# A two-layer language-model tower on one core: in the first attention, the diagonal masks of the key-major scores move from GpSimd to TensorE

## What is computed

```python
Q, K, V = (proj(W_Q), proj(W_K), proj(W_V))        # 8 sequences, 16 heads of 16 features, 512 tokens
Q = _apply_rope(Q, cos, sin)
K = _apply_rope(K, cos, sin)
scores = jnp.einsum('bhsd,bhtd->bhst', Q, K) / jnp.sqrt(jnp.float32(D_K))
scores = jnp.where(causal[None, None], scores, -jnp.inf)
attn = jax.nn.softmax(scores, axis=-1)
out = jnp.einsum('bhst,bhtd->bhsd', attn, V)
```

## Time and profile before

| | us |
|---|---|
| median of 3 runs (lowest to highest) | 1921.43 (1909.6 to 1924.99) |
| the profiled execution, own time | 1921.16 |
| its span, first to last instruction | 1919.4 |
| first attention, PE's first product to the end of the stage | 438.3 (219.3 to 657.6) |
| granted TensorE clock, whole span / this stage | 0.80 / 0.64 of 2.4 GHz |

### The profile page before, as it was taken

One profiled execution on the slowest core, in us unless ns is written; L12 is line 12 of the kernel. 1 busy time (PEld: TensorE's weight loads), 2 busy tenths in 40 slices (PEclk: granted clock), 3 DMA queues, 4 the chain that ended last, 5 costly groups with the idle time before them and its releaser, 6 DMA issues. The chain is left out here.

```text
span 1919.4 us, 30959 instructions
## 1 busy us (share of the span) xinstructions
PE 1405.3 (73%) x9797; PEld 1029.2 (54%) x9798; DVE 956.5 (50%) x1884; ACT 636.3 (33%) x1175; POOL 716.1 (37%) x703
## 2 busy tenths in 40 slices
PE   0599399999999746524442299646599699999997
PEld 0287254444444444423331177544589688888886
DVE  0677665555555254557778255463544233333332
ACT  0177044434344412223221044312233233333332
POOL 6144566656641201113444500200174135454454
PEclk9799566666666777867766599877799899999999
DMA  1034866555531000014323244022011363444431
GB/s 28 18 132 176 238 204 197 162 178 172 191 108 35 7 7 0 0 51 119 99 82 105 63 103 103 10 79 80 6 28 32 113 222 55 114 112 114 112 55 26
DMA packets 123069, 179.31 MB, mean 93 GB/s; under 512 B 26100, under 2 KB 84028, under 8 KB 122980
## 3 DMA queue, kind: packets, MB, share of 16 engines
q1 hardware_dynamic: 94420, 117.25, 20.0%
q0 software_dynamic: 28560, 60.91, 12.3%
HBM read 104.76 MB, written 74.31 MB: 93 GB/s over the span
## 5 line engine op out<-in xcount | busy, mean ns | idle before, releaser
L1378 DVE TENSOR_REDUCE att_top<-att_psS 128x4 f32<-128x512 f32 (+2 forms) x192 | 198.2, 1044 | 176.7 <-PE att_psS L1273 176.0
L1349 ACT ACTIVATE att_prob<-att_psS 128x1024 f32<-128x1024 f32 (+1 forms) x192 | 169.1, 884 | 265.9 <-PE att_psS L1287 265.9
L2427 POOL DMA_INDIRECT out<-ffn1c_y,ffn1c_table x72 | 114.3, 1587 | 181.6 <-ACT ffn1c_y L2540 122.2
L1314 PE MATMUL att_psO<-att_prob,values 128*17 128x512 f32 (+3 forms) x1024 | 146.1, 659 | 10.4 <-ACT att_outT L1355 10.4
L1267 PE MATMUL att_psS<-att_ka,att_qa 48*128 48x384 f32 (+3 forms) x512 | 130.9, 515 | 29.8 <-DMA att_shut<-att_shut 26.1
L1200 POOL TENSOR_SCALAR_AFFINE_SELECT att_prob<-att_prob 128x512 f32<-128x512 f32 x128 | 81.2, 637 | 186.5 <-ACT att_prob L1349 181.4
L1267 PEld LDWEIGHTS att_psS<-att_ka,att_qa 48*128 48x128 f32 x512 | 66.9, 258 | 126.9 <-issue 65.3
L1287 PE MATMUL att_psS<-att_qa,att_ka 50*128 50x256 f32 (+3 forms) x512 | 116.7, 499 | 15.4 <-DVE att_top L1378 13.4
L2568 DVE TENSOR_TENSOR ffn1c_hid<-ffn1c_psG,ffn1c_sil 128x512 f32<-128x512 f32 x72 | 49.8, 691 | 146.0 <-PE ffn1c_psG L2468 146.0
L2468 PE MATMUL ffn1c_psG<-ffn1c_w_h,ffn1c_xh 128*128 x288 | 99.2, 427 | 8.9 <-DMA ffn1c_w_l<-experts_lo 2.9
L2416 POOL DMA_INDIRECT ffn1c_rows<-normed_rows,ffn1c_table x72 | 70.8, 984 | 77.5 <-DVE ffn1c_gate L2588 53.7
(11 more groups left out here) (378 smaller groups left out, 3617.2 us busy)
## 6 DMA issues: line engine op xcount, KB each, us to landing
prep_raw<-in_w_all POOLq DMA_DIRECT2D x27, 512.0 KB, 3.8
experts_hi<-prep_hi POOLq DMA_DIRECT2D x27, 512.0 KB, 4.0
experts_lo<-prep_lo POOLq DMA_DIRECT2D x27, 512.0 KB, 5.7
ffn1c_w_h<-experts_hi SPq DMA_DIRECT2D x8, 1536.0 KB, 6.5
ffn1c_w_l<-experts_lo SPq DMA_DIRECT2D x8, 1536.0 KB, 10.7
qkv_near<-near_keys SPq DMA_DIRECT2D x32, 320.0 KB, 4.4
q_parts<-qkv_part SPq DMA_DIRECT2D x8, 1024.0 KB, 3.9
k_parts<-qkv_part SPq DMA_DIRECT2D x16, 512.0 KB, 5.2
```

The costliest lines, as they stand in the source:

```text
L1314: mm = pe.matmul(psO[VW * h:VW * h + DK + 1, P * j:S], va[:, TG * b + j, :, HG * hg + h], prob[:, w % 2, h, START[j]:START[j] + S - P * j] ...
L1349: act.activation(dst, src, ACT.Exp, scale=0.25).then_inc(s["exp"], 1)
L1378: dve.tensor_reduce(dst, src, AX.X, ALU.max).then_inc(s["max"], 1)
L2427: pool.indirect_dma_start(out=rows_out, in_=y[:, t.buf, :], in_offset=None, out_offset=bass.IndirectOffsetOnAxis(ap=table[:, t.value:t.val ...
```

## The change

- `key_scores` gets mask products of its own: after each pair of score products four products of 64 rows x 128 columns in bf16, `half` against a new constant `sooner`, on the 128 queries of the diagonal block. That is 8 groups of four in a unit, 1,024 products in all, as many as the query side has. POOL's 128 selects and the signal `tri` go; PE's value products wait for the exponential itself.
- The value products have 32 columns in place of 17. They read 15 columns beyond their own, so `va` has one more tile, which POOL clears in `project_rope`; the results of these columns land in rows of `psO` that nobody reads. `psO` need not be cleared any more.
- `half`, `later` (the former `shut`) and `sooner` are made in the identity's block at the program's start, all 128 rows, on POOL: three memsets and six selects. SP's two copies and PE's wait for them go.
- DVE writes the rows of -1 for two buffers ahead of the first round, and for the other four in rounds 0 to 3, two memsets ahead of the maxima of the round.
- POOL's pieces are paced by the maxima: piece u waits for all maxima of unit u - 1.

```diff
-            pool.memset(va[:, :, DK, :], 1.0).then_inc(s["ones"], 1)
+            pool.memset(va[:, NT], 0.0).then_inc(s["ones"], 1)
+            pool.memset(va[:, 0:NT, DK, :], 1.0).then_inc(s["ones"], 1)
...
-            for u in range(NU + 3):
-                if u < n_pieces:
-                    piece(pool, u)
-                v = u - 3
-                if 0 <= v < NU:
-                    for j, through in enumerate((2, 4, 5, 6)):
-                        tri = prob[:, v % 2, :, START[j]:START[j] + P]
-                        pool.wait_ge(s["exp"], 6 * v + through)
-
-                        pool.affine_select(out=tri, in_=tri, compare_op=ALU.is_ge, fill=0.0, base=0,
-                                           pattern=[[0, HG], [1, P]], channel_multiplier=-1).then_inc(s["tri"], 1)
+            for u in range(n_pieces):
+                if u >= 1:
+                    pool.wait_ge(s["max"], 6 * u)
+                piece(pool, u)
...
-            sp.wait_ge(s["mask"], 2)
-            for dst in (half, shut):
-                sp.dma_start(dst[64:128], dst[0:64]).then_inc(s_copied, 16)
...
                     for g in range(2):
                         r = slice(64 * g, 64 * g + QROWS + MROWS)
...
+                    for part in range(2):
+                        for g in range(2):
+                            r = slice(64 * g, 64 * g + 64)
+                            mm = pe.matmul(psS[:, bank, g, col:col + P], half[r, part, :], sooner[r, part, :],
+                                           start=False, stop=True, tile_position=(64 * g, 0), skip_group_check=True)
                 mm.then_inc(s["scoresB"], 1)
...
+            flat = va[:].rearrange("p t d h -> p (t d h)")
...
-                pe.wait_ge(s["tri"], TG * w + j + 1)
+                pe.wait_ge(s["exp"], 6 * w + (2, 4, 5, 6)[j])
...
-                    mm = pe.matmul(psO[VW * h:VW * h + DK + 1, P * j:S], va[:, TG * b + j, :, HG * hg + h],
+                    first = (TG * b + j) * (DK + 1) * H + HG * hg + h
+                    mm = pe.matmul(psO[VW * h:VW * h + VW, P * j:S], flat[:, first:first + VW * H:H],
...
-            pe.wait_ge(s_copied, 32)
-            pe.wait_ge(s["clear"], 1)
...
-            dve.memset(psO[:], 0.0).then_inc(s["clear"], 1)
-            for at in range(LOADED):
+            def minus_rows(at):
                 for g in range(2):
                     dve.memset(ka[64 * g + 32:64 * g + 64, at].bitcast(F32), -1.0).then_inc(s["minus"], 1)
+
+            for at in range(AHEAD):
+                minus_rows(at)
             for u in range(NU + 5):
+                if AHEAD <= u + AHEAD < LOADED:
+                    minus_rows(u + AHEAD)
...
+                for x in marks:
+                    pool.memset(x[:], 0.0).then_inc(s_id, 1)
+                pool.wait_ge(s_id, 5)
+                for g in range(2):
+                    rows = slice(64 * g, 64 * g + 64)
...
+                        pool.affine_select(out=x[rows], in_=x[rows], compare_op=compare, fill=fill, base=0,
+                                           pattern=pattern, channel_multiplier=step).then_inc(s_id, 1)
+                pool.wait_ge(s_id, 11)
```

More of the change, by code:

```diff
@@ L1148, in pair_order, with attend_pairs @@
     return out
-def attend_pairs(nc, q_dram, k_dram, m_dram, ident, va, split):
+def attend_pairs(nc, q_dram, k_dram, m_dram, ident, marks, va, split):
     NU = B * NHG
@@ L1161, in attend_pairs @@
     place = {what[1:]: n for n, what in enumerate(order)}
+    half, later, sooner = marks
     with ExitStack() as ctx:
@@ L1172, in attend_pairs @@
         psO, psM = k.ps("psO", [P, 512]), k.ps("psM", [P, 512])
-        s = {n: k.sem(n) for n in "blank mask minus clear scoresA max topT_ps topT scoresB exp tri pv outT turned rec norm".split()}
+        s = {n: k.sem(n) for n in "minus scoresA max topT_ps topT scoresB exp pv outT turned rec norm".split()}
         s_load = [k.sem(f"load{n}") for n in range(LOADED)]
         s_m_out, s_m_in = ([k.sem(f"{name}{n}") for n in range(2)] for name in ("m_out", "m_in"))
-        s_copied = k.sem("copied")
         block = ctx.enter_context(nc.Block())
@@ L1272, in query_scores @@
                             r = slice(64 * g, 64 * g + 64)
-                            mm = pe.matmul(psS[:, bank, g, col + cols - P:col + cols], half[r, part, :], shut[r, part, :],
+                            mm = pe.matmul(psS[:, bank, g, col + cols - P:col + cols], half[r, part, :], later[r, part, :],
                                            start=False, stop=True, tile_position=(64 * g, 0), skip_group_check=True)
@@ L1286, in key_scores @@
                         r = slice(64 * g, 64 * g + QROWS + MROWS)
-                        mm = pe.matmul(psS[:, bank, g, col:col + cols], ka[r, v % LOADED, q, P * j:P * (j + 1)],
-                                       qa[r, v % LOADED, q, P * j:S], start=True, stop=True, tile_position=(64 * g, 0),
-                                       skip_group_check=True)
+                        pe.matmul(psS[:, bank, g, col:col + cols], ka[r, v % LOADED, q, P * j:P * (j + 1)],
+                                  qa[r, v % LOADED, q, P * j:S], start=True, stop=True, tile_position=(64 * g, 0),
+                                  skip_group_check=True)
+                    for part in range(2):
[3 more added lines that the diff above has]
+                                           start=False, stop=True, tile_position=(64 * g, 0), skip_group_check=True)
                 mm.then_inc(s["scoresB"], 1)
@@ L2615, in tower @@
         ident = k.sb("ident", [P, P])
+        marks = [k.sb(name, [P, 2, P], BF16) for name in ("half", "later", "sooner")]
         s_id = k.sem("ident")
@@ L2632, in _ @@
                                    pattern=[[-1, P]], channel_multiplier=1).then_inc(s_id, 1)
-                pool.wait_ge(s_id, 2)
+                for x in marks:
[3 more added lines that the diff above has]
+                    rows = slice(64 * g, 64 * g + 64)
+                    for x, compare, fill, pattern, step in ((marks[0], ALU.not_equal, 1.0, [[-64, 2], [1, P]], -1),
+                                                            (marks[1], ALU.is_ge, MASKED, [[64, 2], [-1, P]], 1),
+                                                            (marks[2], ALU.is_ge, MASKED, [[-64, 2], [1, P]], -1)):
+                        pool.affine_select(out=x[rows], in_=x[rows], compare_op=compare, fill=fill, base=0,
+                                           pattern=pattern, channel_multiplier=step).then_inc(s_id, 1)
+                pool.wait_ge(s_id, 11)
         embed(nc, res, ident, s_rows, a["ids"], a["E1"], a["tok_w2t"], a["b2"], a["pos"])
-        with nc.sbuf_tensor("values0", [P, NT, DK + 1, H], F32) as va:
+        with nc.sbuf_tensor("values0", [P, NT + 1, DK + 1, H], F32) as va:
             project_rope(nc, res, ident, a["w_qk0"], a["w_v0"], (a["cos"], a["sin"]), q0_dram, k0_dram, va)
```

10 lines of the change are left out of this document (1 added, 9 removed).

## The result

| | kernel before | changed kernel |
|---|---|---|
| median (lowest to highest), us | 1922.69 (1909.6 to 1924.99) | 1858.67 (1858.34 to 1862.87) |
| profiled execution, own time / span | 1921.16 / 1919.4 | 1858.51 / 1856.7 |
| first attention, PE's first product to the end | 438.3 (219.31 to 657.6) | 376.9 (216.38 to 593.3) |
| granted clock, span / this stage | 0.80 / 0.64 | 0.87 / 0.93 |

The ratio is 0.9688, 95% interval 0.9651 to 0.9724: 62.7 us between the two profiled executions.

The account below looks back on a forecast made before the run. PE was taken to bound the first attention, its clock being the largest quantity. From 1921.2 us, -35 (units, clock) - 8 (constants) + 5 (memsets) + 3.5 (identity's block) = -34.5 gave 1887 us, range 1856 to 1917.

Parts of the forecast that it names:

- The bound: First attention: PE bounds it, its clock alternating; the high level is lost at waits for DVE's maxima in steps 5, 0, 1.
- The share at the high level: First attention: 2.4 GHz share rises from 25% to two thirds, units 12.5 us against 13.65, -35 us over 32.
- The forecast's own formula: First attention's mean unit time: 1 / (0.667/11.1 + 0.333/17.0) = 12.5 us, from the high-clock share and unit length at each level.
- the first rival: First attention: masks fill every weak place, full clock throughout, all units 11.1 us, -82 us for units; 1840 us, chance 0.08.
- Unit lengths: First attention, with all masks on the path: 11.1 us a unit at 2.4 GHz, 17.0 at 1.2 GHz; before, 10.47 and 15.2.
- The bounds given for half of the masks hidden: First attention's units, if half of the mask products is hidden: 10.5 us at 2.4 GHz and 16.6 at 1.2 GHz.
- Constants: Start of first attention: PE no longer waits for copies of mask constants, -8 us, or -5 if loads take 6.6 us.
- Memsets: Rounds 1 to 3: DVE's memsets between maxima cost 7.1 us, partly offset by unit 3's load wait; +5 (1.5 to 7).
- The identity's block: Program start: three memsets and six selects ahead of the embedding's gathers, all on the path, +3.5 us.
- POOL, and 32 columns: First attention: removing 128 selects gains 0; value products of 32 columns cost 0, by a 109 ns median weight load elsewhere.
- The old rhythm: First attention: masks thin the value products, high-clock share stays 25%, units 15.0 us, +43 us; 1964 us, chance 0.10.
- The transfers: First attention: faster units wait for loads, 3.18 us every third unit, 35 us, gain gone; about 1920 us, chance 0.08.

Follow-up runs that it names:

- experiments 1 and 3: Changed kernel with POOL's selects back: no key-side mask products, ratio 0.9979; all, 0.9653 (1). Masks in steps 4 and 5 only, 0.9632; steps 0 to 3 only, 0.9883 (3).
- experiment 4: Changed kernel with mask constants made in the projection, 1851.82 us; ten of twelve memsets ahead of round 0, 1848.24; both, 1850.27; unaltered again, 1854.54.
- experiment 1: Changed kernel with POOL's selects and their wait put back: without key-side mask products 1992.1 us, ratio 0.9979; with them 1926.86, ratio 0.9653, both to the kernel before.

## Why the forecast was right, and where it was off

**The bound.** That the clock decides, that it falls at PE's waits for the maxima in steps 5, 0 and 1, and that work put there holds it up was the forecast's argument, and experiments 1 and 3 bear it out. The few falls that are left have another neighbour, which the forecast did not name: in the traces with masks in steps 4 and 5 they lie 0.7 to 1.3 us after a copy that ends a unit, that is within some 0.5 us of the end of PE's wait for that copy (311.84 and the fall at 312.0; 316.30 and one at 316.6). Before, every long low stretch began about 0.5 us ahead of the copy and 1 us behind the start of the product that had waited 0.92 us for the maxima (407.41, the fall at 408.4).

**The share at the high level: the step that was mis-sized.** Two thirds was taken, from the length of the first high stretch; over the 26 steady units it is 96% (three times 3.4 us low in 288.4). The forecast's own formula gives 11.24 us a unit with that, and 11.09 was measured against 12.5. The reason given against the full clock, that 0.7 us of masks does not close an 11 us unit with DVE in series, was an argument on the whole unit. PE at the high level is idle nearly as much as before (10 to 12%, against 13); it is the one wait, 0.92 us to 0.63, that changed with the clock. So the first rival, 1840 us at a chance of 0.08, was in its mechanism nearly what happened, and that the time still lies inside the forecast's range, by 3 us, is in part luck. The rival was too low by 19 us, 4 of them in the other terms and 15 in the units, mostly since the 32 units are not all steady: the first and the last rounds, in which not all three passes run, gained little (+0.8 and -3.8 us). No branch of the forecast had set them apart. On 26 units and the ends, masks and clock gave -64.4 - 3.8 + 0.8 = -67.4 against -35.

The Trainium skill, "TensorE: Matmul & The Clock Gate", section "Why this matters for your kernels", asks for continuous work and no idle gaps. Once the wait was down to 0.63 us the trace came to what that page would give, with gaps that still recur in every unit; and the low stretch of 3.4 us at 277.8 was busy throughout (3.40 of 3.40 us), and those of 20.5 us before nearly so (20.19).

**Unit lengths.** 11.1 us at the high level with all masks on the path; 10.92 was measured. Of the 0.45 us over the 10.47 of before, 0.07 to 0.09 belong to the 32 columns, so 0.38 of the 0.7 us of masks show, those of steps 0 to 3; the groups of steps 4 and 5 are hidden. The bounds given for half of the masks hidden, 10.5 and 16.6, do not follow from the forecast's own terms, which give 10.8 and 16.1; its sum does not use them. The 17.0 us of a whole unit at the low level cannot be read, as none is left. From 12.43 - 10.92 = 1.51 us for 3.4 us at the low level such a unit would take 10.92 / (1 - 1.51 / 3.4) = 19.6 us, an estimate, which may be high since a fall meets PE's fullest part.

**The start.** Constants: -8 (or -5) was forecast, -6.0 came; the last load of unit 0 was issued at 210.18 and PE began at 216.38, so that landing took 5.8 us, not the median 3.9. Memsets: +5 forecast, +6.1 came, all three pairs on the path; experiment 4 gives 3.7 to 5.0 of it back. The wait for unit 3's load went, but not for the reason given, that POOL's pieces no longer run ahead: with the pieces paced as in the changed kernel and the memsets moved, it is back at 2.60 and 3.35 us, so the memsets had only covered it. The identity's block: +3.5 forecast, +3.0 came, 2.8 and 4.8 in experiment 4. PE's first product was forecast near 215 and came at 216.38.

**POOL, and 32 columns.** Both were put at 0. For POOL experiment 1 (selects kept, ratio 0.9653) agrees within the intervals. For the columns the reading failed in its size: the 109 ns came from the second attention, whose 32 columns lie side by side in its tile, while here they lie 16 elements apart, and here the loads went from 113 ns to 146. Whether the distance is the cause was not tried. Most of it is hidden, and 0.07 to 0.09 us a unit shows, 3 us in all. The Trainium skill, "TensorE: Matmul & The Clock Gate", section "LDWEIGHTS (loading the stationary operand)", was quoted as 12.5 ns more a load, 13 us if none were hidden; the loads grew by more, 25 to 33 ns, and the program by less.

**The rivals.** The old rhythm (1964) did not come. The transfers did not become the bound: no wait for a load in the middle of the stage, and POOL's pieces, which now wait for the maxima, sit idle for 120.2 us.

The sum with measured sizes: -67.4 - 6.0 + 6.1 + 3.0 + 1.6 = -62.7, against -34.5. The first term was off by 32.4 us; the others, +0.5 by the forecast and +4.7 measured, take back 4.2.

## What to carry to other kernels

Where PE's clock moves between its levels, look for the wait that recurs ahead of each fall, and price an edit by what it does to that wait; in this case the engine's mean busy share (87% before, 88 to 90 after, at the high level) and the amount of added work said little. Such a suspicion can be tested cheaply by adding products in that place while the work that they are meant to replace stays: here 512 of them ahead of the wait gave a ratio of 0.963, the same number elsewhere 0.988, and none 0.998. Then keep those alone, and count the gain over the rounds that are in the steady state only.

## What the runs showed of the hardware that was not expected

- To add 1,024 products of 128 columns to the engine that bounds the stage took 65 us off the program (1992.1 to 1926.86).
- The low stretches changed in length too: 20.5 us before, 3.4 us with masks in steps 4 and 5, 3.4 and 6.8 us with masks in steps 0 to 3 only, though PE is busy for 96% or more of each that was read. Why they end sooner was not settled; it was not tried to lengthen the products after a fall alone.
- A weight load of a value product took 113 ns in the median with 17 columns that lie 16 elements apart, 146 with 32 such columns, and 109 with the 32 columns side by side of the second attention.
- One and the same program, the kernel before, took 1993.12 us on one chip and 1919.5 to 1922.69 on the others, and the ratios hardly moved with it: 0.9653 and 0.9677 there for two kernels with all masks, 0.9668 and 0.9688 for the changed kernel elsewhere.
